# Two gated cross-attention layers: context beta folded into the latents and a constant row, late products evicted in their own step, zero rows written in pieces

## The reference, cut to what matters

```python
x = x + tanh(g_xattn[0]) * L0_xattn(ctx, layernorm(x), mask, kv_gate, gamma_media, beta_media, gamma_lat, beta_lat, ...)
x = x + tanh(g_ffn[0])   * L0_ffn(layernorm(x), ...)      # 8 experts, two per token
x = x + tanh(g_xattn[1]) * L1_xattn(ctx, layernorm(x), mask, g1, b1, g2, b2, ...)
x = x + tanh(g_ffn[1])   * L1_ffn(layernorm(x), ...)      # quantised, with a convolution over tokens

def L0_xattn(x, latents, ...):                  # x is the context here
    x = layernorm(x, gamma_media, beta_media)
    latents = layernorm(latents, gamma_lat, beta_lat)
    kv = concatenate((x, latents * kv_gate), axis=1)
    q, k, v = latents @ Wq, kv @ Wk, kv @ Wv    # 8 heads of 64
    attn = softmax(mask(q * SCALE @ k.T))
    return (attn @ v) @ Wout
```

## Time and profile before

| | |
|---|---|
| median of 3 runs | 1544.02 us (1532.59, 1544.02, 1547.11) |
| profiled execution, span | 1538.1 us (it has no other time of its own on record) |
| PE busy | 1278.3 us, 83% |
| ACT, DVE, POOL busy | 979.1, 1053.8, 1107.9 us |
| mean granted TensorE clock | 0.937 |
| DMA | 239.96 MB, mean 156 GB/s |

### The profile page before, as it was taken

One profiled execution on the slowest core, in us unless ns is written; L12 is line 12 of the kernel. 1 busy time (PEld: TensorE's weight loads), 2 busy tenths in 40 slices (PEclk: granted clock), 3 DMA queues, 4 the chain that ended last, 5 costly groups with the idle time before them and its releaser, 6 DMA issues.

```text
span 1538.1 us, 45142 instructions
## 1 busy us (share of the span) xinstructions
PE 1278.3 (83%) x16918; PEld 994.2 (65%) x16918; DVE 1053.8 (69%) x2830; ACT 979.1 (64%) x2319; POOL 1107.9 (72%) x1359
## 2 busy tenths in 40 slices
PE   0778787679878989878999999899999999998852
PEld 0556565557667866656887887667676676766642
DVE  4768788977556656665666666777777777877634
ACT  2778787456455666554656566678777777777631
POOL 4768788687557755466777776788878888787653
PEclk9989999879999989989999999999999999999965
DMA  9599997486999954368999997344555444555310
GB/s 314 134 193 235 246 239 174 83 221 188 218 233 252 233 95 97 73 159 171 247 258 231 269 247 181 79 97 98 105 91 94 90 105 94 106 82 91 79 32 6
DMA packets 438329, 239.96 MB, mean 156 GB/s; under 512 B 388848, under 2 KB 420320, under 8 KB 429024
## 3 DMA queue, kind: packets, MB, share of 16 engines
q1 hardware_dynamic: 408216, 178.51, 55.7%
q10 hardware_dynamic: 26824, 51.22, 10.6%
q0 software_dynamic: 3072, 7.34, 1.6%
HBM read 107.78 MB, written 35.50 MB: 93 GB/s over the span
## 4 chain that ended last, share of the span: by engine, by line
PE 39%; ACT 13%; DVE 12%; POOL 11%; issue 9%; DMA 9%; DVEq 3%; SPq 2%; ACTq 1%; POOLq 0%
PE bank_ring L1088 9%; PE bank_ring L1126 6%; PE bank_ring L1074 5%; PE bank_out L1107 5%; DVE scores L1340 4%; DMA expert_up<-experts_up 4%; ACT scores L849 4%; PE bank_x L1187 3%; POOL probs L654 3%; PE bank_scores L1048 3%; ACT probs L856 3%; PE bank_x L1140 3%; DMA probs_turned<-probs 3%; ACT values L876 2%; DMA context<-in_ctx 2%
## 5 line engine op out<-in xcount | busy, mean ns | idle before, releaser
L654 POOL TENSOR_TENSOR probs<-scores,probs 112x487 f16<-112x487 f32 x384 | 425.0, 1123 | 234.2 <-ACT probs L856 229.1
L849 ACT ACTIVATE scores<-scores,score_min 112x487 f32<-112x487 f32 x384 | 265.8, 693 | 121.0 <-DVE score_min L1340 118.2
L1357 DVE SCALAR_TENSOR_TENSOR values<-bank_ring,values 128x512 f16<-128x512 f32 x192 | 132.4, 689 | 216.4 <-ACT values L876 216.3
L1340 DVE CUSTOM_DVE_ANT_0 scores<-bank_scores,mask 112x487 f32<-112x487 f32 x384 | 238.1, 657 | 2.9 <-PE bank_scores L1048 2.9
L856 ACT ACTIVATE probs<-scores 112x487 f16<-112x487 f32 x384 | 214.2, 604 | 24.4 <-DMA probs_turned<-probs 9.0
L1088 PE MATMUL bank_ring<-weights,kv_B 128*128 128x128 f16 x3072 | 198.3, 223 | 1.2 <-DVE keys L1352 1.2
L876 ACT ACTIVATE values<-bank_ring 128x512 f16<-128x512 f32 x192 | 112.9, 588 | 128.9 <-PE bank_out L1107 125.2
L1088 PEld LDWEIGHTS bank_ring<-weights,kv_B 128*128 128x128 f16 x3072 | 187.2, 100 | 10.5 <-DVE keys L1352 2.0
L1107 PE MATMUL bank_out<-values,probs_turned 128*128 128x64 f16 x4608 | 171.9, 195 | 17.7 <-issue 11.4
L1074 PE MATMUL bank_ring<-kv_B,weights 128*128 128x488 f16 x768 | 181.0, 372 | 0.0
L1107 PEld LDWEIGHTS bank_out<-values,probs_turned 128*128 128x128 f16 x4608 | 160.1, 100 | 21.4 <-issue 14.0
(11 more groups left out here) (230 smaller groups left out, 2470.9 us busy)
## 6 DMA issues: line engine op xcount, KB each, us to landing
expert_up<-experts_up SPq DMA_DIRECT2D x43, 1024.0 KB, 5.5
expert_down<-experts_down SPq DMA_DIRECT2D x43, 512.0 KB, 6.6
raw_weights<-in_weights ACTq DMA_DIRECT2D x8, 1536.0 KB, 10.7
experts_up<-expert_up ACTq DMA_DIRECT2D x8, 1024.0 KB, 4.4
raw_weights<-in_weights ACTq DMA_DIRECT2D x6, 1024.0 KB, 8.0
probs_turned<-probs SPq DMA_TRANSPOSE x384
context_turned_B<-kv_B ACTq DMA_DIRECT2D x16, 375.0 KB, 8.7
kv_B<-context_turned_B ACTq DMA_DIRECT2D x16, 375.0 KB, 3.7
```

What stands on the lines that cost most here:

```text
L654: pool.tensor_tensor(PR[:, u % 4, 1, 0:KEYS], S[:, u % 4, 0:KEYS], PR[:, u % 4, 0, 0:KEYS], ALU.subtract).then_inc(probs_split, 1)
L849: act_e.activation(S[:, u % 4, 0:KEYS], S[:, u % 4, 0:KEYS], ACT.Exp, bias=rmin[:, u % 4:u % 4 + 1], scale=-1.0, accum_out=rsum[:, g % 2, ...
L1340: dve.tensor_tensor_reduce(out=S[:, u % 4, 0:KEYS], in0=bS[u % 2][0:TOK, 0:KEYS], in1=mask[:, m, 0:KEYS], scale=1.0, scalar=3.0e38, op0=AL ...
L1357: dve.scalar_tensor_tensor(vN[:, j % 2, 1].rearrange("p t d -> p (t d)"), bank("v", j)[:], 1 / WSCALE, vN[:, j % 2, 0].rearrange("p t d -> ...
```

## The change

**Beta leaves the context.** With beta taken from all rows of the matrix of keys and values, the context needs only gamma·x, and the latents get their own beta less the context's beta (computed once in `scale_gates`). The constant row that this takes from the output is beta through the value and output weights: two new tasks per layer, `v_shift` (24 and 48 products of one column) and `o_shift` (12 and 24 products of 256 columns), in the steps 0, 1 and 61, 62; POOL adds the row to x once per sequence and layer (`shift_row`).

**Context halves from PSUM.** Without beta a low half can be made as gamma·x minus the high half, straight from the bank. ACT makes both layers' high halves from the bank and DVE both low halves; `split_context`, the copy and `context_turned` go. `kv_A` has three slots in place of two. The latents are scaled by ACT from the bank (four activations), and POOL rounds and splits the result, one step earlier than before in layer 0 (`p_lat` itself comes a step later).

**Late products in their own step.** ACT evicts `p_turn`, `p_lat`, `b_lat` and the row of `m_turn` at the end of the step in which PE makes them (`PROMPT`). DVE evicts everything that is late, except `p_turn`, at the end of that step instead of after the masks of the next. `m_turn` becomes a late task.

**Zeros in pieces.** SP writes the zero rows in 12 pieces of at most 4 slots, one in every second step from 2 to 24.

```diff
-            for b in range(2):
-                rows = xs[b].rearrange("(p t) c -> p (t c)", p=128)
...
+            def zero_rows(b, at, n):
+                sp.dma_start(xs[b].rearrange("(p t) c -> p t c", p=128)[:, at:at + n],
+                             xr[:, ZERO_SLOT:ZERO_SLOT + n]).then_inc(rows_zeroed, 16)
...
             for j in STEPS:
+                if j >= ZERO_STEP and j % 2 == 0 and (j - ZERO_STEP) // 2 < ZERO_DMAS:
+                    zero_rows(*ZERO_PIECES[(j - ZERO_STEP) // 2])
```

```diff
+    for layer in range(2):
+        if j == SHIFT_STEPS[layer]:
+            tasks.append(("v_shift", layer))
+        if j == SHIFT_STEPS[layer] + 1:
+            tasks.append(("o_shift", layer))
...
+        if j == 4 * n + 10 and slack(n):
+            tasks.append(("m_turn", n))
-        if j == 4 * n - 6:
+        if j == 4 * n - 5:
             tasks.append(("p_lat", n))
```

ACT:

```diff
                 if name == "p_turn":
                     kb = task[2]
-                    act_e.wait_ge(x1_drained, X1_AT[task])
+                    act_e.wait_ge(x1_filled, X1_AT[task])
+                    if n >= KV_SLOTS[0]:
+                        act_e.wait_ge(v_ready, 4 * (n - 2))
...
+                    for layer in range(2):
+                        c = 8 * layer + V_GAMMA + kb
+                        last = act_e.activation(kv(layer, n)[:, kb, 0, TOK:KEYS], bX1[:, 0:CTX],
+                                                ACT.Identity, scale=vec[:, c:c + 1])
+                    last.then_inc(ctx_hi, 1)
...
+                for t in late(j):
+                    if t[0] in PROMPT:
+                        part(t)
                 if m[2]:
                     round_hidden(m[2][1], m[2][2], m[2][3])
```

POOL, where `split_context` and its calls are gone:

```diff
-                for i, (_, _, c) in enumerate(places):
-                    for kb in range(KB):
-                        scale, shift = latent_vec(c, kb)
-                        last = pool.tensor_scalar(affl[:, i, kb], latT[:, kb], scale, shift, ALU.mult, ALU.add)
+                for i, dst in enumerate(places):
+                    last = pool.tensor_copy(dst[:, :, 0], affl[:, i])
                 after(last)
...
+            def shift_row(layer, n):
+                pool.wait_ge(x1_drained, X1_AT[("o_shift", layer)])
...
+                pool.tensor_tensor(X[:, n], X[:, n], oshift[:], ALU.add).then_inc(row_shifted, 1)
```

DVE:

```diff
+                    dve.wait_ge(ctx_hi, 2 * n + kb + 1)
+                    for layer in range(2):
+                        c = 8 * layer + V_GAMMA + kb
+                        last = dve.scalar_tensor_tensor(kv(layer, n)[:, kb, 1, TOK:KEYS], bX1[:, 0:CTX],
+                                                        vec[:, c:c + 1], kv(layer, n)[:, kb, 0, TOK:KEYS],
+                                                        ALU.mult, ALU.subtract)
+                    last.then_inc(x1_drained, 1)
...
                 for t in late(j - 1):
-                    part(t)
+                    if t[0] == "p_turn":
+                        part(t)
...
                 if halves_in_step(j):
                     split_v(j)
+                for t in late(j):
+                    if t[0] != "p_turn":
+                        part(t)
                 if m[2]:
                     gate_hidden(m[2][1], m[2][2], m[2][3])
```

More of the change, by code:

```diff
@@ L45 @@
 V_GATED = NVEC
+V_LAT_B = NVEC + 2 * KB
 A_STEPS = 4 * NSEQ
@@ L58 @@
 XR_SLOTS = 10
-ZERO_DMAS = sum(-(-t // XR_SLOTS) for t in TILES)
+ZERO_SLOT, ZERO_ROWS = BATCHES[0][1], 4
+ZERO_STEP = 2
+ZERO_PIECES = [(b, at, min(ZERO_ROWS, t - at)) for b, t in enumerate(TILES) for at in range(0, t, ZERO_ROWS)]
+ZERO_DMAS = len(ZERO_PIECES)
 def is_pair(j):
@@ L727, in _ @@
                         rstd("F", n, 1)
-                for t in early(j - 1):
+                for t in early(j - 1) + late(j - 1):
                     if t[0] == "m_turn":
@@ L762, in _ @@
                     split_hidden(m[1], m[2], m[3])
-                if (j + 4) % 4 == 0 and 0 < (j + 4) // 4 < NSEQ:
-                    split_context((j + 4) // 4, 1, 0)
                 if is_pair(j):
                     split_probs(2 * j + 1)
+                for layer in range(2):
+                    for n in range(NSEQ):
+                        if j == row_step(layer, n):
+                            shift_row(layer, n)
                 for b in range(2):
```

240 lines of the change are left out of this document (124 added, 116 removed).

## The result

The changed kernel takes 1557.3 us (median of 20 runs, 1546.5 to 1571.4) and the kernel before, on the same chip, 1544.8 (20 runs). The ratio is 1.0086 with an interval of 1.0063 to 1.0109, from executions within 1.5% of each kernel's fastest: slower by about 13 us, where 5.5 us less was forecast. The profiled execution is the longest of the 20, with a span of 1569.7 us; its own time is 1571.4, 14 us above the median, and where these 14 us lie is shown in the account of the prediction.

What follows compares the result with a forecast made beforehand. No engine was taken as full everywhere: a context load bound the opening, POOL's mask layer 0, a ring of ACT and DVE layer 1. From 1544.0 us, -11.5 - 22 - 4 + 3 + 4 + 25 = -5.5 gave 1538.5, range 1508 to 1566.

Steps and rivals of the forecast that it cites:

- Zeros out of the opening: Opening: without the zero writes the third context loads sooner and DVE's 14.0 us wait goes; -11.5 us.
- Late products in their own step: Layer 1: DVE's evictions now stand before the masks, inside the ring of ACT and DVE; 2.3 us a sequence, +25 us.
- The rival with slack in the ring: Layer 1: PE sets the pace, not ACT and DVE, so evictions cost nothing; -10 for +25, 1503.5 us, chance 0.27.
- Zeros in pieces: Steps 2 to 24: zero writes queue between transposes of probabilities, mostly fitting into free DMA time; +3 us.
- The rival of saturated DMA engines: Steps 0 to 25: DMA limits, zeros cost 13 us, layer 0 gains become waits for turned probabilities; 1574.5 us, chance 0.15.
- Context halves from PSUM, mask early: Layer 0: mask ready a step ahead of PE, so three quarters of its waits come back; -22 us.
- the -4 for X1: Layer 0, 233 to 333 us: the experts' turned row no longer precedes the context copy, freeing X1 sooner; -4 us.
- The constant row's +4: Both layers: extra PE products and POOL additions for the constant row, partly beside idle PE; +4 us.
- its two largest terms: Layer 1 evictions, +25 us (bounds -12.3 and +48), and layer 0's early mask, -22 us (bounds -29.5 and 0).

Runs made afterwards that it cites:

- run 1: Changed kernel with all 12 zero writes issued in the opening, ahead of the steps: 1564.1 us, ratio 1.0132.
- runs 2 and 8: Changed kernel, zeros late (steps 25 to 30): 1559.9 us; the same with `probs` at a multiple of 512 and feed-forward evictions behind the next masks: 1536.3 us.
- runs 9 and 10: Kernel before and changed kernel, each loading 7.9 MB less of expert weights in layer 0: 1533.6 us (0.9929) and 1544.6 us (1.0025).
- run 15: Changed kernel with 7.9 MB less to load and DVE's `norm_out` moved ahead of the masks of its step: 1563.2 us, ratio 1.0126.
- 12: Kernel before with 7.9 MB less to load and 36 of DVE's expert low halves cut to 32 columns: 1530.5 us, ratio 0.9936.
- 13: Changed kernel with 7.9 MB less to load and 36 of DVE's expert low halves cut to 32 columns: 1531.6 us, ratio 0.9926.
- 16: Changed kernel with 7.9 MB less to load, DVE's expert low halves cut, and `norm_out` ahead of the masks: 1552.0 us, ratio 1.0062.
- 18: Changed kernel with 7.9 MB less to load, DVE's expert low halves and ACT's high halves cut to 32 columns: 1538.8 us, ratio 0.9944.
- run 6: Kernel before with two tiny tensors moved so that `probs` lies 64 bytes past a multiple of 512: 1549.2 us, ratio 1.0012.

## Why the prediction was wrong

**Zeros out of the opening: right.** -11.5 forecast, -9.6 measured, and run 1 shows by its 48.1 us that the zeros were the cause.

**Late products in their own step: right.** +25 forecast, +22.1 in steps 105 to 191, and the one move on the kernel before costs 21.1 there. The rival with slack in the ring falls. The 4.4 us per sequence less what ACT waited for PE held: 2.0 us a sequence from these steps, 2.3 forecast.

**Zeros in pieces: +3 forecast, nothing that can be told measured** (runs 2 and 8; their intervals would hide 3 us). The rival of saturated DMA engines named the right symptom, PE waiting for turned probabilities at a share above 1, and the wrong cause: most of these waits are there without the zeros, and both kernels pay some 10 us for the load of the transfers (runs 9 and 10).

**The step that failed is "Context halves from PSUM, mask early":** "three quarters of what PE waits is what such a period can give back: -22", and with it the -4 for X1. The waits did go. The step that contained the wait, in the kernel before (the earlier trace rows have its middle):

```profile
205.00 0.82 PE L1048 MATMUL bank_scores<-keys,queries 64*112 64x488 f16 x6
...
209.21 0.47 PE L1061 MATMUL bank_x<-latents_A,weights 128*128 128x112 f16 x6 [3.38 <-POOL mask L643]
...
213.95 0.86 PE L1107 MATMUL bank_out<-values,probs_turned 128*128 128x64 f16 x24
```

and what DVE did meanwhile:

```profile
204.97 1.26 DVE L1306 SCALAR_TENSOR_TENSOR expert_up<-raw_weights,expert_up 128x512 f16<-128x512 f32 x2
206.15 0.41 DVE L1406 TENSOR_SCALAR x_normed_M<-x,mean_var_M,rstd_M 112x256 f32<-112x256 f32 x1
206.47 0.66 DVE L1352 SCALAR_TENSOR_TENSOR keys<-bank_ring,keys 128x488 f16<-128x488 f32 x1
...
210.59 0.69 DVE L1367 TENSOR_TENSOR wide<-bank_out,prob_sum_inverse 112x512 f32<-112x512 f32 x1
```

The same step of another sequence in the changed kernel, PE:

```profile
174.15 0.82 PE L1049 MATMUL bank_scores<-keys,queries 64*112 64x488 f16 x6
174.91 0.47 PE L1061 MATMUL bank_x<-latents_Q,weights 128*128 128x112 f16 x6
175.22 1.40 PE L1074 MATMUL bank_ring<-kv_A,weights 128*128 128x488 f16 x6
178.11 1.51 PE L1089 MATMUL bank_ring<-weights,kv_A 128*128 128x128 f16 x24 [1.50 <-DVE keys L1384]
181.83 0.51 PE L1108 MATMUL bank_out<-values,probs_turned 128*128 128x64 f16 x12 [2.20 <-issue]
```

and DVE, with POOL's two low halves of probabilities in the last row:

```profile
174.19 2.18 DVE L1338 SCALAR_TENSOR_TENSOR expert_up<-raw_weights,expert_up 128x512 f16<-128x512 f32 x2
176.29 1.19 DVE L1441 TENSOR_SCALAR x_normed_M<-x,mean_var_M,rstd_M 112x256 f32<-112x256 f32 x1
177.40 0.65 DVE L1384 SCALAR_TENSOR_TENSOR keys<-bank_ring,keys 128x488 f16<-128x488 f32 x1
...
181.03 0.69 DVE L1399 TENSOR_TENSOR wide<-bank_out,prob_sum_inverse 112x512 f32<-112x512 f32 x1
```

```profile
174.49 2.84 POOL L669 TENSOR_TENSOR probs<-scores,probs 112x487 f16<-112x487 f32 x2
```

PE no longer waits 3.38 us for the mask. It waits 1.50 us for the low half of the keys and 2.20 us until `norm_out` has emptied bank_out (the profile calls it issue; PE starts 0.11 us after `wide` ends, and the wait vanishes in run 15, where `norm_out` comes first). In the kernel before, both were hidden under the wait for the mask: PE reached the sums 2.7 us after `wide` had ended. The step is 1.3 us shorter to that point (7.68 us for 8.95), not 3.4, and behind it stand the next waits, as the runs with less to load show (9, 10, 12, 13, 15, 16 and 18): whichever of them is removed, by lighter transfers, DVE, ACT, or an earlier `norm_out`, the stage stays between 135 and 145 us. The forecast looked for what is late next in one place only, ACT's roundings of values, and gave 22 of 29.5 us for free. In this step, and in runs 9 and 10 over the stage (15.2 us of waits for the mask gone, 11.0 and 6.9 come), the wait had a second owner.

The -4 seems to have gone the same way. Behind step 24 of the changed kernel the bank of the earlier trace rows is waited for again, now until DVE has made the context's low halves from it:

```profile
PE bank_x L1180 <- DVE kv_B L1627: 5.2, 1, 5.2
...
PE bank_x L1174 <- DVE kv_B L1627: 2.1, 1, 2.1
```

Which chain of engines sets the 135 us isn't settled. What makes single executions differ by 15 us in steps 12 to 20 can be seen: now and then the issue of a DMA takes long, and the engine that issues it stands. In the changed kernel's trace this is the store of a sequence's context, issued by ACT in step 18; PE's long wait behind it is the one of 8.0 us above:

```profile
178.33 14.37 ACTq L802 DMA_DIRECT2D context_turned_B<-kv_B  x1
...
192.80 0.26 ACT L870 ACTIVATE queries<-bank_x 128x112 f16<-128x112 f32 x1 [13.57 <-issue]
```

```profile
193.43 0.74 PE L1061 MATMUL bank_x<-latents_Q,weights 128*128 128x112 f16 x6 [7.98 <-DVE queries L1379]
```

and in the kernel before:

```profile
176.99 4.53 ACTq L794 DMA_DIRECT2D context_turned_B<-kv_B  x1
...
181.62 0.26 ACT L862 ACTIVATE queries<-bank_x 128x112 f16<-128x112 f32 x1 [3.57 <-issue]
```

The same issue takes 16.3 us in run 1 and 4.4 to 4.8 in the other traces with full transfers. With 7.9 MB less to load no issue of ACT in steps 0 to 25 takes over 3.3 us. In run 6 the late ones are SP's two transposes of step 15, 8.8 and 8.9 us to issue (PE waits 12.2 us). Why an issue is now and then three times as long isn't shown. Because of such executions the sum above was made with the medians.

**The sum.** Forecast -5.5, measured about +13. Of the difference of 19 us some 20 are the steps 0 to 105 (-19 forecast with zeros and constant row, +0.8 measured), 2 the opening, and -3 the late products. The constant row's +4 was not measured by itself. The forecast's own range of 1520 to 1562 is slightly off: its two largest terms' bounds, halved, give 1516 at the lower end.

## What to carry to other kernels

A wait in a table is worth only what no other wait covers. Before pricing it, read the step in the timeline and ask of every later instruction of the same engine when its input and its bank would have been ready without the wait. Work set ahead of a hand-over in a ring of two engines costs its length, less what the ring waits elsewhere; one place later, behind the hand-over, the same evictions cost 3.5 us here (524.0 for 520.5) in place of 22. A DMA's issue can hold the engine that issues it; look there when one execution is longer than another. When tensors are added or resized, look at the addresses of what DMAs read.

## What the runs showed of the hardware that was not expected

A transposing DMA cost 8% to 13% more engine time per packet in steps 120 to 184 when the rows it reads started 64 bytes past a multiple of 512 (21.7 and 23.5, 22.8 and 25.1, 20.4 and 23.1 ns per packet in three pairs). Only these two placements were tried, so which multiple it takes isn't shown. The tensor that the DMA writes, `probs_turned`, lies right behind `probs` and moved by the same 64 bytes; no run moved one without the other.

The issue of a DMA held ACT for 4.5 us in the kernel before and for 14.4 us in the changed one, in the stage with expert weights under way; with 7.9 MB less of them no issue of ACT there took over 3.3 us.

DVE can be slower while POOL works on SBUF beside it: two low halves of expert weights took 2.18 us beside POOL's probabilities and 1.26 us beside POOL's latents, and `x_normed_M` 1.19 and 0.41 us (rows above). With latents and mask a step earlier, POOL comes to its probabilities earlier in this step, and DVE pays 1.7 us, just ahead of the keys for which PE waits. Over the whole traces `x_normed` and its kind (lines 1406 and 1441) have a median of 0.40 us alone (6 in the changed kernel), 1.19 beside the probabilities (13), and in the kernel before 0.46 beside the scaling of the latents (6). The expert rows are less plain: one alone takes 0.66 to 0.69 us, beside the probabilities the median of 16 is 0.68 and the longest 1.60, and beside the low half of the latents the median of 12 is 1.10. The Trainium skill (SBUF — State Buffer, section "SBUF: two separate sides") has the rule: a DVE operation with two inputs in SBUF and a GpSimd operation that reads SBUF exclude each other. The slow expert rows agree; that POOL's scaling of the latents, which reads SBUF too, left DVE's two at 1.26 us doesn't fit it as plainly, and no run here took them apart.
